# The first half of the gate/up weights in three pieces and the first half of the down weights in two

## What is computed

```python
xn = _layernorm(x)
s  = _L0_attn_ref(xn, ...)          # 16 query heads, 4 key/value heads of 128, softmax, gelu, layernorm
# feed-forward half, 256 -> 1024 -> 256
gate_up = einsum('bsh,oh->bso', xn, w_gate_up)
gate, up = split(gate_up, 2)
g  = _silu(einsum('bsi,hi->bsh', _silu(gate) * up, w_down))
x  = x + s * g
```

## Time and profile before

| | before |
|---|---|
| median of 3 runs | 622.6 us (621.23 to 622.65) |
| the profiled execution | 623.43 us, of which 621.6 us are the span that the trace covers |
| TensorE matmul busy | 602.3 us, 97% of the span |
| DVE, ACT, POOL busy | 475.0, 431.2 and 299.7 us |
| granted TensorE clock | 0.999 of full speed over the span |

### The profile page before, as it was taken

One profiled execution on the slowest core, in us unless ns is written; L12 is line 12 of the kernel. 1 busy time (PEld: TensorE's weight loads), 2 busy tenths in 40 slices (PEclk: granted clock), 3 DMA queues, 4 the chain that ended last, 5 costly groups with the idle time before them and its releaser, 6 DMA issues.

```text
span 621.6 us, 10684 instructions
## 1 busy us (share of the span) xinstructions
PE 602.3 (97%) x3366; PEld 522.8 (84%) x3366; DVE 475.0 (76%) x1123; ACT 431.2 (69%) x1025; POOL 299.7 (48%) x242
## 2 busy tenths in 40 slices
PE   7999999999899999999999999999999999999984
PEld 5888888888778888888989888888989888888873
DVE  6645555533897778878998788889878988998677
ACT  4434443534988787777987787698787778968752
POOL 1000000000056754554689755458985636587792
PEclk9999999999999999999999999999999999999999
DMA  8700222020388888967497978949798875678741
GB/s 263 254 5 34 69 102 67 1 67 1 121 235 241 254 226 257 244 181 211 135 238 213 290 209 214 248 134 241 194 267 248 214 233 143 193 219 231 211 137 34
DMA packets 66758, 110.01 MB, mean 177 GB/s; under 512 B 7312, under 2 KB 44816, under 8 KB 64656
## 3 DMA queue, kind: packets, MB, share of 16 engines
q1 hardware_dynamic: 66272, 109.02, 61.6%
q10 hardware_dynamic: 432, 0.33, 0.2%
HBM read 64.69 MB, written 44.63 MB: 176 GB/s over the span
## 4 chain that ended last, share of the span: by engine, by line
PE 85%; DVE 5%; DMA 4%; ACT 2%; SPq 1%; issue 1%; POOL 1%; DVEq 0%; ACTq 0%
PE bank L1113 34%; PE down_ps L1113 15%; PE down_ps L1266 13%; PE down_ps L1173 7%; PE bank L1142 7%; PE bank L1140 7%; PE bank L1224 2%; DMA probs<-p_scratch 2%; DMA raw<-in_wd 1%; DMA p_scratch<-probs 1%; POOL pT_lo L680 1%; DVE probs L1053 1%; DVE xn_b L955 1%; ACT probs L812 1%; DVE res L975 1%
## 5 line engine op out<-in xcount | busy, mean ns | idle before, releaser
L680 POOL TENSOR_TENSOR pT_lo<-probs,pT_hi 128x512 fp32r<-128x512 f32 x150 | 191.6, 1298 | 73.1 <-ACT pT_hi L822 72.2
L812 ACT ACTIVATE probs<-probs,least 128x384 f32<-128x384 f32 (+3 forms) x240 | 132.2, 554 | 31.2 <-DVE least L1030 30.4
L707 POOL TENSOR_TENSOR probs<-probs,inv 128x512 f32<-128x512 f32 (+1 forms) x30 | 44.0, 1468 | 142.9 <-DVE inv L1039 142.9
L822 ACT ACTIVATE pT_hi<-probs 128x512 fp32r<-128x512 f32 x150 | 90.9, 627 | 12.0 <-DMA probs<-p_scratch 5.4
L1053 DVE STREAM_TRANSPOSE probs<-probs 128x2048 f32<-128x2048 f32 (+3 forms) x60 | 89.6, 1494 | 1.1 <-POOL probs L707 0.7
L1030 DVE CUSTOM_DVE_ANT_1 probs<-bank,mask 128x256 f32<-128x256 f32 (+2 forms) x180 | 69.6, 419 | 16.3 <-PE bank L1113 10.0
L1266 PE MATMUL down_ps<-wo_lo,cT_hi 128*128 128x256 f32 x256 | 73.5, 287 | 3.2 <-DVE cT_lo L1078 3.2
L1266 PE MATMUL down_ps<-wo_hi,cT_lo 128*128 128x256 f32 x256 | 72.0, 281 | 0.0
L1266 PE MATMUL down_ps<-wo_hi,cT_hi 128*128 128x256 f32 x256 | 71.8, 281 | 0.0
L1113 PE MATMUL bank<-kT_lo,qT_hi 128*128 128x384 f32 (+2 forms) x192 | 66.0, 344 | 2.8 <-DVE least L1030 1.7
L1113 PE MATMUL down_ps<-pT_lo,v_hi 128*128 128x512 f32 x160 | 65.1, 407 | 3.7 <-DVE pT_lo L1073 2.0
(11 more groups left out here) (156 smaller groups left out, 1490.2 us busy)
## 6 DMA issues: line engine op xcount, KB each, us to landing
p_scratch<-probs SPq DMA_DIRECT2D x15, 1024.0 KB, 4.4
probs<-p_scratch SPq DMA_DIRECT2D x60, 256.0 KB, 4.8
p_scratch<-probs SPq DMA_DIRECT2D x15, 768.0 KB, 5.1
probs<-p_scratch SPq DMA_DIRECT2D x60, 192.0 KB, 4.3
inv_b<-i_scratch SPq DMA_DIRECT2D x32, 256.0 KB, 4.9
p_scratch<-probs SPq DMA_DIRECT2D x15, 512.0 KB, 3.0
probs<-p_scratch SPq DMA_DIRECT2D x60, 128.0 KB, 4.7
p_scratch<-probs SPq DMA_DIRECT2D x15, 256.0 KB, 4.7
```

Of the source, the lines that this page charges most:

```text
L680: nc.gpsimd.tensor_tensor(lo[:].rearrange("p (a n) -> p a n", a=BLOCKS), turned(n, t, j), f32(hi[:]).rearrange("p (a n) -> p a n", a=BLOCK ...
L707: nc.gpsimd.tensor_tensor(p, p, factor, ALU.mult).then_inc(probs_made, 1)
L812: nc.scalar.activation(p, p, ACT.Exp, bias=least[:, u, g:g + 1], scale=-1.0, accum_out=total[:, n * T + t, g:g + 1]).then_inc(exp_done, 1)
L822: nc.scalar.activation(hi[:].rearrange("p (a n) -> p a n", a=BLOCKS), turned(n, t, j), ACT.Copy).then_inc(probsT_hi, 1)
```

## The change

Piece 0 becomes three: 128 columns (parts 0, 1), 128 columns (parts 2, 3) and 256 columns (parts 4, 5). Piece 1 becomes chunks 0 and 1 (part 6), chunks 2 and 3 (part 7) and chunks 4 to 7 (part 8). The second gate/up half is parts 9 and 10. The loads are issued, and the parts split, in the order of first use; `DOWN_FIRST` is 6. Two new semaphores, `second_in` and `down_first_in`, let ACT start on the early pieces without waiting for all that shares a buffer.

```diff
-    rest = half - LEAD
+    rest = half - 2 * LEAD
...
-    SPLIT_ORDER = (0, 1, 2, 3, 4, 5, 6, 7)
+    DOWN_FIRST = 3 * DC
+    SPLIT_ORDER = (0, 1, 2, 3, 6, 4, 5, 7, 9, 10, 8)
...
-        order = {(0, 0): 5, (0, 1): 6, (0, 2): 7, (1, 2): 8, (1, 4): 9, (1, 6): 10, (1, 7): 11,
-                 (2, 2): 12, (2, 4): 13, (2, 6): 14, (2, 7): 15, (3, 0): 16, (3, 1): 17}
-        return (order[b, c],) if (b, c) in order else ()
+        order = {(0, 0): (4, 5), (0, 1): (7,), (0, 2): (9, 10), (0, 3): (8,),
+                 (1, 2): (11,), (1, 4): (12,), (1, 6): (13,), (1, 7): (14,),
+                 (2, 2): (15,), (2, 4): (16,), (2, 6): (17,), (2, 7): (18,), (3, 0): (19,), (3, 1): (20,)}
+        return order.get((b, c), ())
...
-        load_piece(0, skip=LEAD_PARTS)
-        load_piece(1)
+        for src, at, _ in pieces[0][LEAD_PARTS:2 * LEAD_PARTS]:
+            sp.dma_start(raw_view(0, at), src).then_inc(second_in, 16)
+        src, at, _ = pieces[1][0]
+        sp.dma_start(raw_view(1, at), src).then_inc(down_first_in, 16)
+        load_piece(0, skip=2 * LEAD_PARTS)
+        load_piece(1, skip=1)
...
-        sp.wait_ge(part_split, split_at(3))
+        sp.wait_ge(part_split, split_at(5))
         load_piece(2)
...
         high(2, 3)
+        high(DOWN_FIRST)
         gate_part(0, 0)
-        high(4)
...
         low(2, 3)
+        low(DOWN_FIRST)
         hid_part(0, 0)
-        low(4)
...
-            if first and c in (1, FC // 2):
-                pe.wait_ge(part_split, split_at({1: 3, FC // 2: 7}[c]))
+            if first and c in (1, 2, FC // 2):
+                pe.wait_ge(part_split, split_at({1: 3, 2: 5, FC // 2: 10}[c]))
...
-            if first and c in (0, FC // 2):
-                pe.wait_ge(part_split, split_at(4 if c == 0 else 5))
+            if first and c in (0, 2, FC // 2):
+                pe.wait_ge(part_split, split_at({0: DOWN_FIRST, 2: 7, FC // 2: 8}[c]))
```

More of the change, by code:

```diff
@@ L415, in build @@
     x_in, lead_in, clock_tile = sem("x_in"), sem("lead_in"), sem("clock_tile")
+    second_in, down_first_in = sem("second_in"), sem("down_first_in")
     ident_loaded, const_in = sem("ident_loaded"), sem("const_in")
@@ L465, in gate_up_cols @@
         return w[:, c, :].rearrange("p (g n) -> p g n", g=2)[:, :, lo:lo + n]
[L467 to L472, removed]
+    pieces.append([(wgu_v[:, c, :, i * LEAD:(i + 1) * LEAD], ((i * DC + c) * 2 * LEAD, 2 * LEAD, 2),
+                    [gate_up_cols(w, i * LEAD, LEAD, c) for w in wgu_s]) for i in range(2) for c in range(DC)]
+                  + [(wgu_v[:, c, :, 2 * LEAD:half], (DC * 4 * LEAD + c * 2 * rest, 2 * rest, 2),
+                      [gate_up_cols(w, 2 * LEAD, rest, c) for w in wgu_s]) for c in range(DC)])
+    pieces.append([(wd_v[:, i:i + n, :], (i * D, n * D, n),
+                    [w[:, i:i + n, :] for w in wd_s]) for i, n in ((0, 2), (2, 2), (4, 4))])
     pieces.append([(wgu_v[:, c, :, half:F], (c * 2 * half, 2 * half, 2),
@@ L513, in parts, with landed @@
                 n += 1
-    def landed(eng, k, lead=False):
-        if lead:
+    def landed(eng, n, k):
+        if n < LEAD_PARTS:
             eng.wait_ge(lead_in, 16 * LEAD_PARTS)
[L519 to L523, removed]
+        elif n < 2 * LEAD_PARTS:
+            eng.wait_ge(second_in, 16 * LEAD_PARTS)
+        elif n == DOWN_FIRST:
+            eng.wait_ge(down_first_in, 16)
+        else:
+            loaded, start = (raw_in, 0) if k < FFN_PIECES else (attn_in, FFN_PIECES)
+            apart = (2 * LEAD_PARTS, 1)
+            eng.wait_ge(loaded[k % RAW_SLOTS], 16 * sum(
+                len(pieces[i]) - (apart[i] if i < 2 else 0)
+                for i in range(start, k + 1) if i % RAW_SLOTS == k % RAW_SLOTS))
     def turned_back(i, t, q):
@@ L731, in high @@
                 if n in which:
-                    landed(act, k, n < LEAD_PARTS)
+                    landed(act, n, k)
                     nc.scalar.activation(hi, raw_view(k, at), ACT.Copy).then_inc(part_hi, 1)
```

## The result

| | before | changed |
|---|---|---|
| median of 12 runs | 622.62 us (621.23 to 624.52) | 625.15 us (623.85 to 626.34) |
| ratio, 95% interval | | 1.0029 (1.0018 to 1.0041) |
| the profiled execution | 623.43 us, span 621.6 | 625.14 us, span 623.4 |

The change makes the kernel slower by 0.29%, or 1.8 us on 622.62 with an interval of 1.1 to 2.6. The forecast was +0.4 us with a range of -1.2 to +2.0 around the 622.6 shown then: the direction, a small loss, is right, and its size is over four times what I gave. Put on the 622.6 of the forecast the ratio gives 624.4, just inside 621.4 to 624.6. The two medians alone stand 2.5 us apart, and 625.15 lies 0.55 above that range. I go by the ratio, which is what was measured again (1.0027 in experiment 6).

A forecast was written before the change was run, and what follows sets the result against it. TensorE was taken as the bound, with 1.7 us won at the front; W of 5.6 and DVE's L + 12.33 put row 1's transposes 0.4 us later than before, so 622.6 + 0.4 = 623.0 us, range 621.4 to 624.6.

The forecast's parts named there:

- The bound and the front: TensorE bounds the kernel; of 1.8 us lost around the first chunks, the smaller early loads win 1.7 us.
- Loads of the small pieces, SP's additional issues: At the start: small pieces land before they are needed; three more issues cost SP about 0.6 us each, nobody waits.
- Piece 2 free at 15.76: In `raw[0]`: DVE finishes parts 4 and 5 at 15.76, so piece 2 can be issued 2.8 us later than before.
- DVE's queue behind the landing: From piece 2's landing, DVE's steps in order set the transposes of row 1 at L + 12.33.
- L: Landing of piece 2, when ACT starts its first high part; forecast 15.76 + 5.6 = 21.4.
- W: Time from the first issue of piece 2 to the landing of its second load; taken as 5.6 us, ends 4.8 and 7.0.
- the sign of being wrong: At piece 2: the forecast is wrong if ACT starts on it before 20.7 or after 23.
- A: Rival: the front's gain gets through, transposes of row 1 at 31.6, -1.7 us, 620.9 us; chance 6%.
- B: Rival: piece 2 loads quickly (W 4.9 or less) and the floor holds, -0.3 to -0.5 us, 622.2 us; chance 20%.
- C: Rival: the token load behind piece 2 mixes with it, W 8.2, transposes at 36.3, +3.0 us, 625.6 us; chance 12%.
- D: Rival: at the front the small pieces land late and `gate_up(0, 1)` waits as before, some 624.2 us; chance 4%.
- Nothing else is late: Behind row 1's transposes: `wk`, `wv` and later tokens come in time; additional instructions cost below 0.2 us each.

The follow-up runs named there:

- experiment 6: Two runs: the changed kernel again, ratio 1.0027 to before; and the changed kernel with row 2's token load held back until piece 2 landed, 1.0009.
- e2: Changed kernel with the first load of piece 2 issued once parts 0 to 3 are split; ratio 0.9994 to the kernel before.
- e7: Changed kernel with row 2's token load held back until piece 2 has landed; ratio 1.0009 to the kernel before.
- Experiments 1 to 3: Changed kernel with part 8 split after chunk 1 (1.0008), with piece 2's first load issued early (0.9994), with both (0.9984, again 0.9973).
- e6: The changed kernel measured again without edits, on another chip; ratio 1.0027 to the kernel before.
- e5: Changed kernel with three additional matmuls (0.70 us) between `gate_up_first` and `gate_up(0, 1)`; ratio 1.0017 to the kernel before.
- e3: Changed kernel with part 8 split after chunk 1 and the first load of piece 2 issued early; ratio 0.9984 to the kernel before.
- e8: Changed kernel with part 8 after chunk 1 and piece 2's first load early, measured again on another chip; ratio 0.9973 to the kernel before.

## Why the prediction was right, point by point

- **The bound and the front**: right. 1.8 us were to be had, 1.7 forecast, 1.53 came: chunk 1 started 0.08 later than its 11.83, as the first product did (9.02 for 8.95), and `down(0, 0)` started at 14.80 and not at 14.66. That step was called just in time and was 0.1 late.
- **Loads of the small pieces, SP's additional issues**: right. Nothing waited for them.
- **Piece 2 free at 15.76**: SP issued it at 15.89.
- **DVE's queue behind the landing**: right to 0.13 us. L + 12.33 was forecast, L + 12.20 measured in three executions of different L (21.77, 22.78, 22.99), and 12.18 and 12.19 in e2 and e7. Experiments 1 to 3 show its two causes: part 8 in front of the statistics, and the load. Each mended alone brings the total back to about that of the kernel before (1.0008 and 0.9994), and only both together win.
- **W is the term that was mis-sized.** 5.6 was taken and 6.7 is the average of four profiles; the first one, 5.9, is the quickest. The rows used were those of a pair with nothing behind it (5.2) and of a pair with one load behind it (5.9), and I went between them. The row of this very pair before the change, 7.0, had the token load behind it as well, and I set it aside because of what was in front. With nothing in front but the tail of one table (`rowc` landed at 16.9, so "those are gone by 15.76" was not quite so), the pair still took 6.7, and 5.5 once the token load was held back, near the 5.2 of the empty queue. With W = 6.7 the sum would have read L = 22.5, transposes at 34.8, +1.5 us, and the measured ratio says +1.8 (1.1 to 2.6).
- **What was luck.** +1.8 us is near the upper end of the range (+2.0), and 0.29% is a hair inside the 0.3% that was given 81%. The range holds it because it was drawn out to W = 7.0, not because 5.6 was a good choice. That ACT started on piece 2 at 21.77, close to 21.4, is luck too: in e6 and e5 it was 22.78 and 22.99, and 23 was the sign of being wrong.
- **The rivals.** A (the gain gets through) is false for the change as made, though its arithmetic is what e3 and e8 reach once the order is mended: 31.7 where 31.6 was given. B (quick loads) is what e2 approaches, at 33.16. C, the token load behind piece 2 delaying it, is at work, at a W of 6.7 and not of 8.2, though the mixing that C names explains only the end of it (experiment 6). D did not happen.
- **The rule** from the Trainium skill, "DMA: Bandwidth & Descriptors", section "Anatomy of one DMA", would have given W 4.4. No trace agrees: piece 2 without the load behind it took 5.5, the `wq` pair 5.2, and the quickest pair of 512 KB loads, `wk` and `wv` in e5, 4.9. It was right not to use it here.
- **"Nothing else is late"**: right as far as it can be told. The shift of 0.70 alone costs -0.6 to +1.0 us. The average shift of the changed kernel at the transposes (34.8 against 33.3 and 33.9 in the two profiles with the unchanged front) is 0.9 to 1.5 us. Whether the rest up to 1.8 is anything but spread isn't settled; the interval of 1.1 to 2.6 doesn't ask for it.

## What to carry to other kernels

Splitting a load so that its first user starts sooner moves the whole buffer's timetable: ask when the buffer is free for the next piece, and what stands on the in-order engine behind the point where that piece is now waited for. Follow the chain to the next thing that TensorE needs from that engine (here the normalised tokens of the next row, at L + 12.2), not only to the wait that goes. Put each rounding step where its engine has idle time before the item it would delay, and reuse part of a buffer as soon as that part is free. And where an urgent load comes late, look at what is queued right behind it, not only ahead of it: here holding that load back was worth about 1 us. Last, one profile is one value: L moved by 1.2 us between executions, and a theory priced from the quickest of them (experiment 2) gets the mechanism right and the total wrong.

## What was new about the hardware

A DMA queued **behind** an urgent pair on the same queue can go with a later landing of that pair: two loads of 512 KB landed 5.5 us after the first issue when nothing followed (one execution), and 5.9 to 7.2 us (6.7 on average over four) with a third load of 512 KB issued 1.25 us behind the first. It isn't a rule: another pair of 512 KB, with two such loads issued from 0.9 us behind its first, landed after 4.9 to 5.2 us in four executions. What makes the difference is open. The same load varies by 1.3 us between executions of kernels that load alike up to there, and a kernel whose wait hangs on it varies with it.
